# A four-engine attention and feed-forward kernel: every round of the second half gets its own order of scores, tiles, sums, jobs and evictions

## The chip, the cores and the metric

One core of one Trainium2 chip runs the whole program in one launch. The metric is the device time of that core in microseconds (us). TensorE (PE) multiplies, VectorE (DVE), ScalarE (ACT) and GpSimd (POOL) do elementwise work, SyncE (SP) issues nearly all DMAs.

## The reference

```python
x = L0_attn_X                       # (4, 1024, 256)
xn = _layernorm(x, axis=-1)
s = _L0_attn_ref(xn, Wq, Wk, Wv, Wo)    # 16 heads of 16, RoPE, causal softmax over 1024 keys
g = _silu(_L0_ffn_ref(xn, ...))         # Hadamard, 256 -> 2 x 1024, silu(gate) * up, Hadamard, -> 256
x = x + s * g
```

## The kernel before, in words

The first block (about 236 us) normalises the input, makes Q, K and V for all 4096 tokens and does the first part of the feed-forward. The second block (about 569 us) does attention and the rest of the feed-forward, woven together. This text is about the second block.

**Units.** Attention is cut into 16 units, one per batch and group of four heads. A unit takes 5 rounds (`NR`), and there are 85 rounds `z` in all: 5 that only compute maxima for unit 0, 75 in which the scores of one unit stand beside the maxima of the next, and 5 at the end with scores alone. The round's place in its unit is `r = z % 5`.

**What a round holds.** Two steps of a unit (a step is one or two blocks of 128 keys against 512 queries, at most). For each step there are two `scores`, one for each pair of heads: two matmuls side by side in the array (64 rows each), into a pair of PSUM banks. ACT takes their exponential into `probs` (`exponentials`, L1564). Then `weigh` (L1413) multiplies the probabilities by the values: four heads side by side, 32 columns of the array each, all summed in bank 7. Four `max_tile` (48 rows, L1368, some with a mask added on L1379) compute scores of the next unit whose maxima DVE reads (`read_tile`, L1681 and L1686). One or two jobs of the feed-forward (`gate`, `up`, a quarter of `down`, L343 and L353), each six matmuls on the full array, or others (`piece`, `turn`). Twice a unit, `rows` (L1426) transposes the maxima.

I name the four scores of a round S0 to S3 (S0 and S1 are the two of its first step), its tiles T0 to T3, its sums V0 (the second step of the round before) and V1 (this round's first step), its jobs J0, J1, ..., and `rows` R. The array has thus three ways in which it is divided: by rows (S and T), by columns (V), undivided (J and R). Every score, tile and job waits until the previous user of its bank has been read (`wait_banks`).

**Who is read where.** Bank 7 collects the sums of the first 512 queries (steps 0 to 2), is copied to `o_raw` by ACT (`take_heads`, L1607), and then collects those of the other 512 (steps 3 to 9). The first sum into it waits for that copy:

```python
if js[0] == 0 and QC * u + c:
    pe.wait_ge(o_taken, QC * u + c)
```

Step 2 is weighed by V1 of the round with r = 1, step 3 by V0 of the round with r = 2. So between these two sums stands one copy on ACT. Each engine goes through its list in order: an instruction that waits holds all that stands behind it.

**Orders and banks.** Six banks form three pairs (`PAIR_A`, `PAIR_B`, `PAIR_C`) for scores and tiles; jobs use single banks of a pair or bank 6. Before, the order on PE is the same in all full rounds (S0 T0 S1 V0 T1 S2 T2 J.. S3 T3 V1, with S2 ahead of T1 at r = 4), which pair each takes is fixed, ACT and DVE have orders written out in their own loops. In a round with r = 2, ACT's loop begins with `take_heads`, ahead of the exponentials.

Of the kernel before, what the change touches and what calls it, by code (L numbers as in the profile page):

```python
# [166 lines left out]

todo = []
# [5 lines left out]
SLOTS, FIRST_SLOTS, LAST_SLOTS = ((1, 1, 1, 2, 2), (4,) * NR, (1, 2, 0, 0, 0))  # L174
slots_at = lambda z: (FIRST_SLOTS if z < NR else LAST_SLOTS if z >= END else SLOTS)[z % NR]
# [30 lines left out]
PAIR_A, PAIR_B, PAIR_C = ((0, 1), (2, 3), (4, 5))  # L206
KEPT = 6
pair_of, bank_of, before_of = ({}, {}, {})

scores_first = lambda z: z % NR == NR - 1 and steps_at(z) and tiles_at(z)  # L210
holder = {bank: None for bank in range(7)}

LAST_EARLY = jobs_in(LAST, PLACES - 1)[-1]
holder[early_bank[LAST_EARLY]] = LAST_EARLY


def give(what, banks):
    before_of[what] = [x for m, x in enumerate(holder[b] for b in banks) if x and x not in [holder[b] for b in banks[:m]]]
    for bank in banks:
        holder[bank] = what  # L220


kept_open = False
for z in range(NROUND):
    if z == END + 2:
        give(('late heads', NU - 1, QC - 1), (LATE_HALVES[1][0],))

    jobs = jobs_at[z]
    if len(jobs) > 1 and jobs[0][0] == 'rows':
        jobs[0], jobs[1] = (jobs[1], jobs[0])  # L230

    if steps_at(z):
        jobs.sort(key=lambda j: j[0] == 'turn')
    now, tiles = (steps_at(z), [('tile', *t) for t in tiles_at(z)])
    s0, s1 = ([('scores', now[0], now[1] + n, p) for p in range(2)] if now else [] for n in range(2))
    early = len(jobs) if now else len(jobs) // 2

    one, other = (PAIR_B, PAIR_A) if z == NR else (PAIR_A, PAIR_B)
    for what, banks in zip(s0 + s1, (one, PAIR_C, one if scores_first(z) else other, other) if tiles
                           else (PAIR_A, PAIR_B, PAIR_A, PAIR_B)):  # L240
        pair_of[what] = banks
    pair_of.update(zip(tiles, (other, other if scores_first(z) else one, PAIR_C, PAIR_C) if now
                       else (PAIR_B, PAIR_C, PAIR_B, PAIR_C)))
    behind = s1[:1] + tiles[1:2] if scores_first(z) else tiles[1:2] + s1[:1 if tiles else 2]
    for what in s0[:1] + tiles[:1] + s0[1:] + behind + tiles[2:3 if now else 2]:
        give(what, pair_of[what])
    spare = list(one) if tiles else [4, KEPT] if z < NROUND - 1 else [KEPT, 4]
    ends_kept = kept_open or any(j[0] == 'down' for j in jobs)
    for m, j in enumerate(jobs):
        if m == early:  # L250
            for what in tiles[2:]:
                give(what, pair_of[what])
        if turn_of(j) not in bank_of:
            if j[0] == 'down' or (j[:2] != ('piece', LAST - 1) and (m == 0 or (not now and m == 3)) and not ends_kept):
                bank = KEPT
            else:
                bank = spare[0]
                spare.reverse()
            assert bank != KEPT or not kept_open
            bank_of[turn_of(j)] = bank  # L260
            give(turn_of(j), (bank,))
        if j[0] == 'down':
            kept_open = not ends_turn(j)
# [718 lines left out]
def second_block(nc, ps, io, scr, sh):  # L982
# [5 lines left out]
    with ctx:  # L988
# [69 lines left out]
        pair_round = lambda n, ib: max(job_round.get((kind, n, ib), -1) for kind in ('gate', 'up'))  # L1058

        ups = lambda z: [j for j in jobs_at[z] if j[0] in ('gate', 'up') and z == pair_round(*j[1:])  # L1060
                         and (j[0] == 'up' or ('up', *j[1:]) not in jobs_at[z])] if z >= 0 else [
                             j for j in jobs_in(LAST, PLACES - 1) if j[0] == 'up']
# [17 lines left out]
        def _(eng):  # L1080
# [95 lines left out]
            for z in range(NROUND):  # L1176
# [157 lines left out]
        def _(pe):  # L1334
# [169 lines left out]
            for z in range(NROUND):  # L1504
                now, tiles = (steps_at(z), tiles_at(z))
                if now:
                    u, s = now
                    scores(u, s, 0)
                if tiles:
                    max_tile(*tiles[0])  # L1510
                if now:
                    scores(u, s, 1)
                    if s:
                        weigh(u, s - 1)
                    elif u:
                        weigh(u - 1, NS - 1)
                if scores_first(z):
                    scores(u, s + 1, 0)
                for t in tiles[1:2]:
                    max_tile(*t)  # L1520
                if now and not scores_first(z):
                    scores(u, s + 1, 0)
                if now:
                    if not tiles:
                        scores(u, s + 1, 1)
                    for t in tiles[2:3]:
                        max_tile(*t)
                if z == NROUND - 1:
                    end_piece(0, 0)
                for m, j in enumerate(jobs_at[z]):  # L1530
                    if not now and m == len(jobs_at[z]) // 2:
                        for t in tiles[2:]:
                            max_tile(*t)
                    job(j)
                if now and tiles:
                    scores(u, s + 1, 1)
                    for t in tiles[3:]:
                        max_tile(*t)
                if now:
                    weigh(u, s)  # L1540
# [14 lines left out]
        def _(act):  # L1555
# [76 lines left out]
            for z in range(NROUND):  # L1632
                u, r = (z // NR - 1, z % NR)
                now = steps_at(z)
                if now and r == 2 and u < NU - 1:
                    take_heads(u, 0)
                if now:
# [11 lines left out]
                if now:
                    exponentials(now[0], now[1] + 1, 0)  # L1650
                for j in jobs_at[z]:
                    job(j)
                if now:
                    exponentials(now[0], now[1] + 1, 1)
# [13 lines left out]
        def _(dve):  # L1668
# [122 lines left out]
            for z in range(NROUND):  # L1791
                tiles = tiles_at(z)
                jobs = jobs_at[z]
                ahead = 3 if steps_at(z) else 2
                early = len(jobs) if steps_at(z) else len(jobs) // 2
                for t in tiles[:ahead]:
                    read_tile(*t)
# [5 lines left out]
                if z == 0:  # L1803
                    dve.memset(q_s[1][:, :, :, :].bitcast(F32), 0.0)
                for j in jobs[:early]:
                    job(j)
                for t in tiles[ahead:]:
                    read_tile(*t)
                if z == 0:
                    dve.memset(k_s[1][:, :, :, :].bitcast(F32), 1.0).then_inc(ones_set, 1)  # L1810
                for j in jobs[early:]:
                    job(j)
# [76 lines left out]
```

## Time and profile before

| what | value |
|---|---|
| time, median of 3 runs | 804.46 us (803.2 to 804.69) |
| span of the profiled execution | 804.6 us |
| busy PE / DVE / ACT / POOL | 787.2 / 566.7 / 497.8 / 411.1 us |
| first block, up to the first tile | 235.7 us |
| the 75 full rounds | about 509 us |

The profile lists the span, not another time for its own execution; the span agrees with the median within 0.02%. PE's busy time counts each matmul until its result has drained, while the next one already streams, so 98% busy doesn't mean that nothing can be gained or lost: what tells is the distance from one matmul's start to the next.

### The profile page before, as it was taken

The numbers are of one execution on the slowest core, as the hardware profiler recorded it, in microseconds if no ns is written. First come the engines' busy times: TensorE is split into PE (matmuls) and PEld (weight loads), VectorE is DVE, ScalarE is ACT, GpSimd is POOL, SyncE is SP. The second block draws the span as 40 slices with busy tenths as digits, with TensorE's granted clock in tenths as the row PEclk, the third lists the DMA queues.
The fourth block names the chain that finished last, engine by engine and source line by source line (L and its number), as shares of the span: only waits on it lengthen the run. The fifth ranks groups of instructions, "written<-read, shape, count | busy, mean of one in ns | idle before, by whom it ended". The sixth has DMA issues, their size and how long they took to land. (4 is left out here: it accounts for less than half of the span.)

```text
span 804.6 us, 14554 instructions
## 1 busy us (share of the span) xinstructions
PE 787.2 (98%) x5232; PEld 482.7 (60%) x5232; DVE 566.7 (70%) x1021; ACT 497.8 (62%) x686; POOL 411.1 (51%) x472
## 2 busy tenths in 40 slices
PE   8999999999999999999999999999999999999987
PEld 4678788888766555555555555555555555555545
DVE  5875545456686777777777777777777777777736
ACT  4576355463544777667777665677766677666472
POOL 3878678574742463321765434267453236746233
PEclk9999999999999999999999999999999999999997
DMA  9262444354541222333333453334344333445121
GB/s 319 84 199 96 158 156 158 106 131 145 182 113 39 65 77 60 91 107 107 103 107 110 122 171 93 95 108 132 115 114 142 98 105 95 133 130 170 67 87 70
DMA packets 61248, 95.71 MB, mean 119 GB/s; under 512 B 10553, under 2 KB 27641, under 8 KB 61177
## 3 DMA queue, kind: packets, MB, share of 16 engines
q1 hardware_dynamic: 59176, 92.42, 38.0%
q10 hardware_dynamic: 2000, 2.36, 0.9%
q8 instruction: 42, 0.69, 0.4%
q14 instruction: 30, 0.24, 0.1%
HBM read 57.54 MB, written 36.95 MB: 117 GB/s over the span
## 5 line engine op out<-in xcount | busy, mean ns | idle before, releaser
L1564 ACT ACTIVATE probs<-ps 128x1024 f32<-128x1024 f32 (+1 forms) x320 | 292.0, 938 | 93.7 <-PE ps L1391 92.0
L1686 DVE TENSOR_REDUCE mx<-ps 128x4 f32<-128x1024 f32 (+1 forms) x192 | 216.1, 1134 | 58.9 <-PE ps L1368 37.2
L1249 POOL TENSOR_SCALAR_AFFINE_SELECT probs<-probs 128x256 f32<-128x256 f32 (+1 forms) x192 | 92.6, 485 | 255.1 <-ACT probs L1564 254.5
L1681 DVE CUSTOM_DVE_ANT_0 ps<-ps,tri 128x512 f32<-128x512 f32 (+1 forms) x256 | 153.8, 652 | 48.4 <-PE ps L1368 48.3
L1413 PE MATMUL ps<-probs,v_ones 128*32 128x512 f32 (+3 forms) x1584 | 157.0, 486 | 0.1
L1391 PE MATMUL ps<-q_s,k_s 64*128 64x512 f32 (+3 forms) x768 | 143.7, 399 | 3.8 <-ACT probs L1564 1.4
L1368 PE MATMUL ps<-k_s,q_s 48*128 48x512 f32 (+3 forms) x768 | 134.7, 381 | 4.1 <-DVE mx L1686 0.8
L1391 PEld LDWEIGHTS ps<-q_s,k_s 64*128 64x128 f32 x768 | 67.0, 184 | 103.9 <-issue 53.6
L1368 PEld LDWEIGHTS ps<-k_s,q_s 48*128 48x128 f32 x768 | 69.5, 185 | 63.6 <-ACT probs L1564 38.2
L343 PE MATMUL ps<-xh,wug_hi 128*128 128x512 f32 x256 | 105.6, 413 | 1.0 <-DVE rot L898 1.0
L398 POOL TENSOR_TENSOR a_sb<-a_sb,u_sb 128x512 f32<-128x512 f32 x64 | 82.4, 1295 | 41.7 <-ACT u_sb L371 20.9
L343 PE MATMUL ps<-xl,wug_hi 128*128 128x512 f32 x256 | 100.1, 391 | 0.0
L343 PE MATMUL ps<-xh,wug_lo 128*128 128x512 f32 x256 | 100.1, 391 | 0.0
L411 POOL TENSOR_TENSOR hid_lo<-a_sb,hid_hi 128x512 fp32r<-128x512 f32 x64 | 83.4, 1314 | 3.5 <-ACT hid_hi L828 3.1
L384 DVE SCALAR_TENSOR_TENSOR a_sb<-a_sb,ps 128x512 f32<-128x512 f32 x64 | 43.7, 684 | 47.6 <-ACT a_sb L363 47.6
L363 ACT ACTIVATE a_sb<-ps,half_gate 128x512 f32<-128x512 f32 x64 | 44.1, 688 | 46.5 <-PE ps L343 35.6
L371 ACT ACTIVATE u_sb<-ps,half_both 128x512 f32<-128x512 f32 x64 | 44.0, 687 | 37.0 <-PE ps L343 35.7
L1413 PEld LDWEIGHTS ps<-probs,v_ones 128*32 128x32 f32 x1584 | 35.4, 108 | 45.1 <-issue 36.9
L343 PEld LDWEIGHTS ps<-xh,wug_hi 128*128 128x128 f32 x256 | 48.0, 187 | 23.6 <-issue 13.7
L353 PE MATMUL ps<-hid_hi,wd_hi 128*128 128x512 f32 x128 | 54.1, 423 | 0.6 <-POOL hid_lo L411 0.4
L343 PEld LDWEIGHTS ps<-xh,wug_lo 128*128 128x128 f32 x256 | 48.1, 188 | 10.7
L343 PEld LDWEIGHTS ps<-xl,wug_hi 128*128 128x128 f32 x256 | 48.2, 188 | 8.3
(151 smaller groups left out, 1061.5 us busy)
## 6 DMA issues: line engine op xcount, KB each, us to landing
scr_qk<-kinds SPq DMA_DIRECT2D x64, 256.0 KB, 2.4
q_s<-scr_qk SPq DMA_DIRECT2D x64, 128.0 KB, 2.8
k_s<-scr_qk SPq DMA_DIRECT2D x64, 128.0 KB, 3.0
scr_heads<-o_raw SPq DMA_DIRECT2D x30, 256.0 KB, 2.1
scr_v<-v_st SPq DMA_DIRECT2D x16, 256.0 KB, 2.9
q_s<-scr_qk SPq DMA_DIRECT2D x64, 64.0 KB, 3.0
k_s<-scr_qk SPq DMA_DIRECT2D x64, 64.0 KB, 3.1
v_raw<-scr_v SPq DMA_DIRECT2D x16, 256.0 KB, 2.8
```

Of the source, the lines that this page charges most:

```text
L343: last = pe.matmul(ps[:, bank, :], w[:, d, cols], a[:, d, :], start=m == 0, stop=m == len(terms) - 1)
L353: last = pe.matmul(ps[:, bank, :], w[:, ib, cols], h[:, ib, :], start=ib == 0 and k == 0, stop=ib == IB - 1 and k == 2)
L363: act.activation(sh.a_sb[:, m % NA, :], ps[:, bank, :], ACT.Tanh, scale=sh.half_gate[:, ib:ib + 1]).then_inc(sh.t_ok, 1)
L398: pool.tensor_tensor(sh.a_sb[:, m % NA, :], sh.a_sb[:, m % NA, :], sh.u_sb[:, m % NUP, :], op=ALU.mult).then_inc(sh.hid_ok, 1)
L411: pool.tensor_tensor(sh.hid_lo[:, ib, :], sh.a_sb[:, m % NA, :], sh.hid_hi[:, ib, :].bitcast(F32), op=ALU.subtract).then_inc(sh.hl_ok, 1)
L1249: pool.affine_select(out=part, in_=part, compare_op=ALU.is_ge, fill=0.0, base=0, pattern=pattern, channel_multiplier=-1).then_inc(cut, 1)
L1368: last = pe.matmul(ps[:, banks[e], n * w:(n + 1) * w], q[rows, i // TPC, p, i % TPC * P:(i % TPC + 1) * P], keys[rows, part, p, 0:w], star ...
L1391: last = pe.matmul(ps[:, banks[e], col:col + w], k_s[u % 2][rows, j // TPC, p, j % TPC * P:(j % TPC + 1) * P], q_s[u % 2][rows, c, p, q0:C ...
L1413: last = pe.matmul(ps[VW * h:VW * (h + 1), bank, lo:queries.stop], v_ones[u % 2][:, j, h, :], probs[:, nth_step(u, s) % 2, h // 2, h % 2, ...
L1564: act.activation(probs[:, n % 2, p, :, 0:w], ps[:, bank:bank + 2, 0:w], ACT.Exp, scale=SCALE).then_inc(exp_ok, 1)
L1681: last = dve.tensor_tensor_reduce(part_of, part_of, sh.tri[:, CH - w:CH], 1.0, LOWEST, ALU.add, ALU.max, mx[:, v % 2, kind, h, i % TPC:i % ...
L1686: last = dve.tensor_reduce(out[:, :, pairs[0]:pairs[0] + n], ps[:, banks[0]:banks[0] + 2, 0:n * w].rearrange('p e (x k) -> p e x k', x=n), ...
```

## The change

The order of every round is now a string, one for each place `r` in the unit, and one loop on each engine follows it. PE's list is the string itself. ACT's and DVE's lists are made from it: scores, rows, turns and heads go on ACT's list where they stand in the string, tiles, turns and pieces on DVE's; the evictions of gate, up and down go on ACT's list one item later and on DVE's two items later (`ACT_LAG`, `DVE_LAG`). `H` is ACT's copy of bank 7. Each score or tile takes the pair of banks that by a table of assumed durations has been free longest, and each job the bank that has. GpSimd's and SP's conditions follow the new lists. Rounds of maxima alone keep their order. `EXTRA` adds a slot only in rounds that don't occur in this size. The work, the number of matmuls and the distribution of jobs over rounds are the same.

```diff
+ORDER_F = (
+    'S0 T0 H T1 V0 S1 S2 J0 T2 J1 J2 R S3 V1 T3 J3',
+    'S0 S1 T0 V0 T1 S2 T2 H J0 R T3 S3 J1 J2 V1 J3',
+    'S0 T0 S1 V0 H T1 S2 T2 J0 T3 J1 S3 V1 J2 J3 R',
+    'S0 T0 H S1 V0 T1 S2 T2 J0 R S3 J1 T3 J2 J3 V1',
+    'S0 T0 S1 V0 T1 S2 T2 J0 J1 S3 T3 R J2 V1 J3',
+)
+ORDER_END = 'S0 S1 V0 R H S2 S3 J0 J1 J2 J3 V1'
+ACT_LAG = 1
+DVE_LAG = 2
...
+TIMES = {'tile': (220, 1500), 'scores': (220, 1400), 'gate': (1390, 600), 'up': (1390, 1400), 'weigh': (850, 0), 'rows': (60, 600),
+         'turn': (440, 1800), 'piece': (1400, 900), 'down': (1400, 2200), 'divide': (500, 1200), 'end piece': (600, 0)}
...
+def oldest(sets):
+    return min(sets, key=lambda banks: max(freed[b] for b in banks))
...
+        if what[0] in ('scores', 'rows', 'turn', 'heads'):
+            acts.append(what)
+        if what[0] in ('tile', 'turn', 'piece', 'divide'):
+            dves.append(what)
...
+        elif kind == 'H':
+            if now[1] == 4 and now[0] < NU - 1 or now[1] == 0 and now[0]:
+                new.append(('heads', now[0] - (now[1] == 0), int(now[1] == 0)))
...
             for z in range(NROUND):
                 u, r = (z // NR - 1, z % NR)
                 now = steps_at(z)
-                if now and r == 2 and u < NU - 1:
-                    take_heads(u, 0)
-                if now:
-                    for p in range(NPAIR):
-                        exponentials(*now, p)
-                if r == 0 and u >= 1:
-                    take_heads(u - 1, 1)
...
+                for m, what in enumerate(act_of[z]):
+                    if what[0] == 'scores':
+                        exponentials(*what[1:])
...
+                    elif what[0] == 'heads':
+                        take_heads(*what[1:])
```

**Place one: ACT, around the start of the round with r = 2.** `u_sb` is the eviction of a job, `probs` the exponential of one score, `o_raw0` the copy of bank 7 after step 2, `a_sb` again a job, `shift` the eviction of R. Before:

```order
L371 ACTIVATE u_sb<-ps,half_both 128x512 [waits hid_ok,up_ok]
L1564 ACTIVATE probs<-ps 128x1024 [waits pv_ok,scored]
L1607 COPY o_raw0<-ps 128x512 [waits o_out01,pv_ok]
L1564 ACTIVATE probs<-ps 128x1024 [waits pv_ok,scored] x3
L363 ACTIVATE a_sb<-ps,half_gate 128x512 [waits hl_ok,gate_ok]
L1571 ACTIVATE shift<-ps 16x128 [waits row_in01,mt_ok]
```

And now:

```order
L459 ACTIVATE u_sb<-ps,half_both 128x512 [waits hid_ok,up_ok]
L1624 ACTIVATE probs<-ps 128x1024 [waits pv_ok,scored] x3
L1667 COPY o_raw0<-ps 128x512 [waits o_out01,pv_ok]
L1624 ACTIVATE probs<-ps 128x1024 [waits pv_ok,scored]
L451 ACTIVATE a_sb<-ps,half_gate 128x512 [waits hl_ok,gate_ok]
L1624 ACTIVATE probs<-ps 128x1024 [waits pv_ok,scored]
L1631 ACTIVATE shift<-ps 16x128 [waits row_in01,mt_ok]
```

The copy has moved from ahead of S0's and S1's exponentials to behind both.

**Place two: PE at the same point.** The scores S0, the tile T0 (with its mask), the scores S1, and V0, which waits for the copy (`o_taken`). Before:

```order
L1391 MATMUL ps<-q_s0,k_s0 128x512 [waits tile_read]
L1391 MATMUL ps<-q_s0,k_s0 128x512
L1368 MATMUL ps<-k_s1,q_s1 128x256 [waits exp_ok]
L1368 MATMUL ps<-k_s1,q_s1 128x256 x3
L1379 MATMUL ps<-mask,one_hot 128x2x128 x4
L1391 MATMUL ps<-q_s0,k_s0 128x512 [waits tile_read]
L1391 MATMUL ps<-q_s0,k_s0 128x512
L1413 MATMUL ps<-probs,v_ones0 32x512 [waits o_taken,exp_ok]
```

And now:

```order
L1476 MATMUL ps<-q_s0,k_s0 128x512 [waits tile_read]
L1476 MATMUL ps<-q_s0,k_s0 128x512
L1453 MATMUL ps<-k_s1,q_s1 128x256 [waits tile_read]
L1453 MATMUL ps<-k_s1,q_s1 128x256 x3
L1464 MATMUL ps<-mask,one_hot 128x2x128 x4
L1476 MATMUL ps<-q_s0,k_s0 128x512 [waits exp_ok]
L1476 MATMUL ps<-q_s0,k_s0 128x512
L1498 MATMUL ps<-probs,v_ones0 32x512 [waits o_taken,exp_ok]
```

PE's own order here is unchanged; only whose read a bank waits for differs.

**Place three: PE, from the end of the round with r = 0 into that with r = 1.** The tile T3 of r = 0 is the pair of `128x384` on the first line below; V1 is `32x512`, S0 is the first `128x256`, and the tile T0 of r = 1 is the `128x128`. Before:

```order
L1368 MATMUL ps<-k_s1,q_s1 128x384 [waits tile_read]
L1368 MATMUL ps<-k_s1,q_s1 128x384
L1413 MATMUL ps<-probs,v_ones0 32x512 [waits v_set,o_taken,cut,exp_ok]
L1413 MATMUL ps<-probs,v_ones0 32x512 x3
L1391 MATMUL ps<-q_s0,k_s0 128x256 [waits tile_read,shift_ok]
L1391 MATMUL ps<-q_s0,k_s0 128x256
L1391 MATMUL ps<-q_s0,k_s0 128x128 x2
L1368 MATMUL ps<-k_s1,q_s1 128x128 [waits exp_ok,qk_in11]
```

And now (V1 stands first, T3 behind it):

```order
L1498 MATMUL ps<-probs,v_ones0 32x512 [waits v_set,o_taken,cut,exp_ok]
L1498 MATMUL ps<-probs,v_ones0 32x512 x3
L1453 MATMUL ps<-k_s1,q_s1 128x384 [waits exp_ok,shift_ok]
L1453 MATMUL ps<-k_s1,q_s1 128x384
L1476 MATMUL ps<-q_s0,k_s0 128x256 [waits tile_read]
L1476 MATMUL ps<-q_s0,k_s0 128x256
L1476 MATMUL ps<-q_s0,k_s0 128x128 x2
L1476 MATMUL ps<-q_s0,k_s0 128x256 [waits exp_ok]
L1476 MATMUL ps<-q_s0,k_s0 128x256
L1476 MATMUL ps<-q_s0,k_s0 128x128 x2
L1453 MATMUL ps<-k_s1,q_s1 128x128 [waits tile_read,qk_in11]
```

T3 has moved behind V1, S1 ahead of T0, and T0 now waits for a tile's read (`tile_read`), that of this same T3, whose pair it takes, where it waited for an exponential.

## Rows read from the trace of the kernel before

**Rows 1.** The page: busy us, share of the span, instructions.

```profile
PE 787.2 (98%) x5232; PEld 482.7 (60%) x5232; DVE 566.7 (70%) x1021; ACT 497.8 (62%) x686; POOL 411.1 (51%) x472
```

**Rows 2.** Windows: us, busy time of each engine, PEclk, DMA share, GB/s.

```profile
235.70:253.70 18.00, 16.47 (x75) 11.43 (x74) 12.68 (x26) 4.44 (x8) 0.00 (x0) 0.91 0.18 59
253.70:763.00 509.30, 505.05 (x3782) 270.67 (x3782) 388.75 (x738) 348.05 (x454) 236.68 (x315) 1.00 0.37 107
```

**Rows 3.** Timeline of PE alone, tile and scores into a job.

```profile
302.18 0.41 PE L1391 MATMUL ps<-q_s,k_s 64*128 64x512 f32 x2
302.41 0.40 PE L1368 MATMUL ps<-k_s,q_s 48*128 48x512 f32 x2
302.74 0.50 PE L343 MATMUL ps<-xh,wug_hi 128*128 128x512 f32 x1
303.08 0.39 PE L343 MATMUL ps<-xl,wug_hi 128*128 128x512 f32 x1
303.31 0.39 PE L343 MATMUL ps<-xh,wug_lo 128*128 128x512 f32 x1
```

**Rows 4.** Timeline of PE's weight loads at the same place.

```profile
302.26 0.19 PEld L1368 LDWEIGHTS ps<-k_s,q_s 48*128 48x128 f32 x2
302.74 0.19 PEld L343 LDWEIGHTS ps<-xh,wug_hi 128*128 128x128 f32 x1 [0.29 <-issue]
302.85 0.19 PEld L343 LDWEIGHTS ps<-xl,wug_hi 128*128 128x128 f32 x1
```

**Rows 5.** Timeline, start of a round with r = 2.

```profile
366.36 0.50 PE L1391 MATMUL ps<-q_s,k_s 64*128 64x512 f32 x2
366.50 0.59 ACT L1607 COPY o_raw<-ps 128x512 f32<-128x512 f32 x1 [0.22 <-PE ps L1413]
366.98 1.95 ACT L1564 ACTIVATE probs<-ps 128x1024 f32<-128x1024 f32 x2
367.28 0.50 PE L1391 MATMUL ps<-q_s,k_s 64*128 64x512 f32 x2
367.71 1.07 PE L1413 MATMUL ps<-probs,v_ones 128*32 128x512 f32 x8
...
368.70 0.50 PE L1368 MATMUL ps<-k_s,q_s 48*128 48x512 f32 x2
```

**Rows 6.** Timeline, a score whose exponential starts on an idle ACT.

```profile
373.09 0.50 PE L1391 MATMUL ps<-q_s,k_s 64*128 64x512 f32 x2
373.62 1.94 ACT L1564 ACTIVATE probs<-ps 128x1024 f32<-128x1024 f32 x2 [0.56 <-PE ps L1391]
```

**Rows 7.** Timeline, T3 of a round with r = 0 and its read.

```profile
358.90 0.44 PE L1368 MATMUL ps<-k_s,q_s 48*128 48x384 f32 x2
359.38 0.57 DVE L1681 CUSTOM_DVE_ANT_0 ps<-ps,tri 128x384 f32<-128x384 f32 x1 [0.54 <-PE ps L1368]
359.86 0.60 DVE L1681 CUSTOM_DVE_ANT_0 ps<-ps,tri 128x384 f32<-128x384 f32 x1
360.38 0.14 DVE L1681 DVE_READ_ACCUMULATOR2_ANT mx<- 128x1 f32 x1
```

**Rows 8.** Waits, whole span: us in total, times, longest.

```profile
PEld ps L1368 <- DVE mx L1686: 7.5, 24, 1.0
PEld ps L1391 <- DVE mx L1681: 6.4, 20, 0.6
PEld ps L1368 <- DVE mx L1681: 2.9, 8, 0.9
PEld ps L1391 <- DVE mx L1686: 2.6, 9, 0.4
```

**Rows 9.** Windows before and in the one stretch of a lower clock.

```profile
238.00:239.00 1.00, 0.50 (x2) 0.19 (x2) 1.00 (x4) 0.31 (x1) 0.00 (x0) 1.00 0.70 262
239.00:240.00 1.00, 0.55 (x3) 0.36 (x4) 1.00 (x4) 0.00 (x0) 0.00 (x0) 1.00 0.05 8
241.00:242.00 1.00, 1.00 (x4) 0.81 (x3) 1.00 (x2) 0.00 (x0) 0.00 (x0) 0.50 0.79 268
```

More of the change, by code:

```diff
@@ L203 @@
 LAST_FEATURES = max(z for j, z in job_round.items() if j[0] in ('gate', 'up'))
-PAIR_A, PAIR_B, PAIR_C = ((0, 1), (2, 3), (4, 5))
+PAIRS = [(0, 1), (2, 3), (4, 5)]
+PAIR_A, PAIR_B, PAIR_C = PAIRS
 KEPT = 6
 pair_of, bank_of, before_of = ({}, {}, {})
-scores_first = lambda z: z % NR == NR - 1 and steps_at(z) and tiles_at(z)
-holder = {bank: None for bank in range(7)}
+holder = {bank: None for bank in range(8)}
 LAST_EARLY = jobs_in(LAST, PLACES - 1)[-1]
 holder[early_bank[LAST_EARLY]] = LAST_EARLY
+freed = {bank: 0 for bank in range(8)}
+freed[early_bank[LAST_EARLY]] = 1500
+TIMES = {'tile': (220, 1500), 'scores': (220, 1400), 'gate': (1390, 600), 'up': (1390, 1400), 'weigh': (850, 0), 'rows': (60, 600),
+         'turn': (440, 1800), 'piece': (1400, 900), 'down': (1400, 2200), 'divide': (500, 1200), 'end piece': (600, 0)}
+clock = 0
 def give(what, banks):
@@ L220, in give, with until @@
         holder[bank] = what
+def oldest(sets):
+    return min(sets, key=lambda banks: max(freed[b] for b in banks))
+def until(banks, kind):
+    for b in banks:
+        freed[b] = clock + sum(TIMES[kind])
+order_of, act_of, dve_of = ([], [], [])
+late_act, late_dve = ([], [])
 kept_open = False
 for z in range(NROUND):
+    now, tiles = (steps_at(z), tiles_at(z))
+    v, r = divmod(z, NR)
     if z == END + 2:
         give(('late heads', NU - 1, QC - 1), (LATE_HALVES[1][0],))
-    jobs = jobs_at[z]
@@ L229 @@
[L229 to L263, printed above, removed]
@@ L264 @@
-    if not jobs and not now:
-        for what in tiles[2:]:
-            give(what, pair_of[what])
-    if now:
-        for what in (s1[1:] if tiles else []) + tiles[3:]:
-            give(what, pair_of[what])
+    rows = [j for j in jobs_at[z] if j[0] == 'rows']
+    others = [j for j in jobs_at[z] if j[0] != 'rows']
+    if now:
+        others.sort(key=lambda j: j[0] == 'turn')
+    shape = ORDER_T[r] if not now else ORDER_END if not tiles else ORDER_F[r]
+    order, acts, dves = ([], [], [])
@@ new lines, in take @@
+    def take(what):
+        order.append(what)
+        for late in (late_act, late_dve):
+            for x in late:
+                x[0] -= 1
+        for late, to in ((late_act, acts), (late_dve, dves)):
+            while late and late[0][0] <= 0:
+                to.append(late.pop(0)[1])
+        if what[0] in ('scores', 'rows', 'turn', 'heads'):
+            acts.append(what)
+        if what[0] in ('tile', 'turn', 'piece', 'divide'):
+            dves.append(what)
+    turn_pairs = [PAIR_A, PAIR_B]
@@ new lines @@
+    order_of.append(order)
+    act_of.append(acts)
+    dve_of.append(dves)
+assert not late_act and not late_dve
+gated_round = {what: z for z in range(NROUND) for what in dve_of[z] if what[0] in ('gate', 'down')}
+taken_round = {what: z for z in range(NROUND) for what in act_of[z] if what[0] in ('up', 'gate')}
+pool_round = {}
+for j in list(taken_round):
+    if j[0] == 'up':
+        pool_round[j] = max(taken_round[j], gated_round.get(('gate', *j[1:]), 0))
+assert sum(j[0] == 'down' for z in range(END, NROUND) for j in jobs_at[z]) <= 3
@@ L1056, in second_block @@
         block = ctx.enter_context(nc.Block())
[L1058 to L1062, printed above, removed]
+        ups = lambda z: sorted([j for j, at in pool_round.items() if at == z], key=lambda j: nth_hid(*j[1:])) if z >= 0 else [
+            j for j in jobs_in(LAST, PLACES - 1) if j[0] == 'up']
         nth_x = lambda n: n - NEARLY - 1
@@ L1504, in _ @@
             for z in range(NROUND):
-                now, tiles = (steps_at(z), tiles_at(z))
-                if now:
[L1507 to L1540, printed above, removed]
+                for what in order_of[z]:
+                    if what[0] == 'tile':
+                        max_tile(*what[1:])
+                    elif what[0] == 'scores':
+                        scores(*what[1:])
+                    elif what[0] == 'weigh':
+                        weigh(*what[1:])
+                    elif what[0] == 'end piece':
+                        end_piece(*what[1:])
+                    elif what[0] != 'heads':
+                        job(what)
             end_piece(0, 1)
@@ L1634, in _ @@
                 now = steps_at(z)
-                if now and r == 2 and u < NU - 1:
-                    take_heads(u, 0)
-                if now:
-                    for p in range(NPAIR):
-                        exponentials(*now, p)
-                if r == 0 and u >= 1:
-                    take_heads(u - 1, 1)
-                if at(z, 'high') is not None and at(z, 'high') < LAST - 1:
-                    high_part(at(z, 'high'))
                 if z < NR:
                     normalise_at(z)
-                if z < NR:
                     for j in ups(z - 1):
                         hidden_high(*j[1:])
[L1649 to L1654, printed above, removed]
+                n_scores = 0
+                for m, what in enumerate(act_of[z]):
+                    if what[0] == 'scores':
+                        exponentials(*what[1:])
+                        n_scores += 1
+                        if n_scores == 2 and at(z, 'high') is not None and at(z, 'high') < LAST - 1:
+                            high_part(at(z, 'high'))
+                    elif what[0] == 'heads':
+                        take_heads(*what[1:])
+                    else:
+                        job(what)
                 if z == NR:
@@ L1802, in _ @@
                     low_part(LAST - 1)
[L1803 to L1812, printed above, removed]
+                for n, what in enumerate(dve_of[z]):
+                    if what[0] == 'tile':
+                        read_tile(*what[1:])
+                    else:
+                        job(what)
+                    if z == 0 and n == 1:
+                        dve.memset(q_s[1][:, :, :, :].bitcast(F32), 0.0)
+                    if z == 0 and n == 3:
+                        dve.memset(k_s[1][:, :, :, :].bitcast(F32), 1.0).then_inc(ones_set, 1)
                 if z == NR:
```

77 lines of the change are left out of this document (68 added, 9 removed), and 5 rows, old and new, of the table ORDER_T.

## The prediction, made before the changed kernel ran

> **What bounds the kernel now.** The page first: PE is busy 98% of the span, DVE 70%, ACT 62%, POOL 51% [rows 1]. The windows say where: in the 75 full rounds, 509.3 us, PE is busy 505.05 us and its clock is granted in full [rows 2]. Busy there is no proof of work, because a matmul counts until it has drained. So I went to the timeline and read starts. Inside a job, matmuls start every 0.23 us (303.08, 303.31); a tile behind a score also follows at 0.23 us (302.18, 302.41), its load under the matmul ahead [rows 3, 4]. Where the division of the array changes, from the tile to the job, the next start comes after 0.33 us, and the one behind it after 0.34 us [rows 3]. The load explains it: the job's first load starts together with its first matmul at 302.74, instead of under the one before, while the second load already starts at 302.85, under the first matmul [rows 4]. So one change of division costs 0.10 + 0.11, about 0.2 us.
>
> The order lists 491 such changes in the second block, 447 of them in the full rounds: 447 x 0.2 = 89 us of 509. What else is lost on PE are waits for a read bank. Those that DVE ends sum to 7.5 + 6.4 + 2.9 + 2.6 = 19.4 us in 61 waits, none over 1.0 us [rows 8]; part of each is the load that would have been late anyway. Streaming alone I estimate at 388 us for these rounds (the columns in the order, at 0.23 us for 512, and 0.80 for a V of 512, which is the 1.0 us from 367.71 to the next start at 368.70 [rows 5] less one change). 509 - 388 - 89 leaves 32 us for waits of every size. That is the most an order can win back. PE's list is therefore the bound, and other engines matter where PE waits for them.
>
> **The change, part by part.** Three things differ on PE: how often the division changes, which read each item waits for, and when the reads come.
>
> *Changes of division.* In an ordinary unit the old order changes 6 times in each of the five rounds, 30 in all. The new strings give 9, 5, 7, 8 and 6, so 35: at r = 0 a tile stands behind the job and R stands alone behind that tile, at r = 2 R stands behind V1, at r = 3 the second job is parted from the first. Over the whole program I count 571 for 491: 80 more, x 0.2 us [rows 3] = **+16 us**. Nothing hides this, since it lies on PE itself. The Trainium skill, page "TensorEngine Tiling (Array Packing)", section "Key Properties", says that changing the tiling mode drains the TensorE. If a change exposed a whole drain and load, the price from rows would be (0.39 - 0.23) + 0.19 = 0.35 us [rows 3, 4] and the part 28 us; the starts in the trace show 0.2, and the sum goes by them.
>
> *The copy of bank 7.* On PE, V0 at r = 2 is the first sum into bank 7 after the copy. Today the copy starts at 366.50, 0.14 us after S0, and has ended at 367.09; V0 starts at 367.71, 1.35 us after S0, and doesn't feel it [rows 5]. In the new ACT list the copy stands behind the exponentials of S0 and S1. With S0 at 0: its exponential begins at 0.53, which is the distance from a score to its exponential on an idle ACT (373.09 to 373.62) [rows 6]; two exponentials take 1.95 [rows 5], so the copy begins at 2.48 and ends at 3.07; with 0.1 for the semaphore V0 starts at 3.17. 3.17 - 1.35 = 1.82 us, and V0 has nothing to go past it: T1, S2, T2 and the job stand behind it on PE. This comes in units 0 to 14 (the last unit's copy is DVE's and stays), 15 x 1.82 = **+27 us**. The store of the heads (SP) starts some 2.4 us later; their loads stand rounds away, so I cost it at nothing, and if one did wait it would be ACT's next copy in the same bank of `o_raw`, five rounds on.
>
> *The tile T0 at r = 1.* Today T3 of r = 0 is followed by V1, S0, and T0 takes the pair of a score; it is S1 that takes T3's pair. In the new order T3 is behind V1, then S0 and S1 of the next round take the two older pairs, and T0 is left with T3's. In the trace, that tile starts at 358.90, DVE reads it from 359.38 to 360.52 in two passes [rows 7]: 1.62 us from start to free, and 0.05 to PE, 1.67. In the new order T0 would start after T3 itself (0.17 for 384 columns, 0.11 for its late load) and two scores of 384 columns (0.17 each, as r = 1 uses step 2): 0.62. So PE waits 1.05 us, and the load after such a wait is late too (0.11). 15 times 1.16 = **+17 us**. It holds if DVE is at T3 when it arrives: T2 and the gate's eviction stand ahead of it, and the string puts 2 us of PE work (R, S3, V1) between T2 and T3. V0 is queued behind T0; its exponentials are done by then, so nothing is late beyond PE.
>
> *The waits that go.* The old tile T3 waited for T2's pair, two places back, and similar tiles now wait for T1's. At r = 3 and 4 little is waited for before or after. The 19.4 us of [rows 8] lie mostly in the rounds with r = 0 and 1. And each of the two new waits lets DVE and ACT catch up. I take **-12 us**, between 0 and the 32 us above, nearer to the part of [rows 8] that isn't late load.
>
> *At nothing.* R at r = 2 goes behind V1, so its eviction on ACT and the two small DMAs on SP go about 2 us later; the scores that need those rows are two rounds, some 13 us (509.3 / 75 each), away, and that SP order also holds the next unit's load, which has as long. R at r = 0 keeps its distance to the scores that need it. ACT's job evictions stand one item later, DVE's gates about where they stood, and POOL, at 236.68 busy of 509.30 [rows 2], has room for what it gets later; if it had none, V1's mask step would hold PE. Rounds of maxima and the first block don't change. More instructions on the lists than before: none that compute.
>
> **Sum.** Against the profiled execution's span of 804.6 us (the median is 804.46, the same within the measurement): 804.6 + 16 + 27 + 17 - 12 = 852.6, so **852 us**, 6% slower.
>
> **The rivals.**
> - *Forecast: both waits and the changes are paid.* 840 to 866 us. Chance 0.60.
> - *One new wait is smaller than it looks.* If DVE reads T3 at once and waits of every size go, T0's 17 us vanish: 804.6 + 16 + 27 - 32 = 816 at the least, and 836 with 12 won back. For it: the old waits are all short [rows 8]. Against it: a bank cannot be written before 1.67 us, and 0.62 us of work stands between. Chance 0.17, 816 to 840.
> - *The clock falls.* The one stretch with half the clock in the second block comes behind two slices in which PE was busy 0.50 and 0.55 [rows 9]. The wait at r = 2 leaves PE idle for about 1.8 us in 3.2. Around that stretch the clock's mean over 18 us is 0.91 [rows 2], so the dip cost 0.09 x 18 = 1.6 us of work. In all 15 units that gives +24, 876 us; in some, 866 to 876. Against it: the new stalls are shorter than that dip's and stand between full stretches. Chance 0.16.
> - *Other side: not slower.* Only if the copy is no wait. The point is 1.35 us after S0: if the copy ends by then, V0 doesn't notice. That needs ACT to be done with both exponentials 0.8 us after S0, while one takes 0.97 [rows 5]; or PE to be so late at V0 for another reason that the wait is covered. With T0's wait covered too and all 32 us won back, 804.6 + 16 - 32 = 789 us. Chance 0.05.
> - *The evenly spread order wins as much as it costs* (16 + 27 + 17 = 60 against at most 32): would need twice the waits that there are. Chance 0.02, about 804.
>
> **How the numbers follow.** The forecast is that of the likeliest case, 852. The range takes the case with one smaller wait down to 830 and that of the clock up to 874; about 2 in 10 is left outside. A measurement here tells 0.2% (1.6 us) from no change. Faster by more: 0.05; within: 0.02; slower: 0.93.
>
> **What the changed profile would show.** Copy: in a round with r = 2, the `o_raw` copy behind a pair of exponentials, and V0 about 3.2 us after S0; among PE's waits a new group ended by ACT's copy, 15 times, each up to 1.8 us. Tile: a group ended by DVE's second pass over a 384-column tile, 15 times, about 1 us. Changes: the distance of 0.33 where the job or R is parted from its like. Rounds: r = 2 longer by 1.6 to 2 us, r = 1 by about 0.5 to 1, r = 0 by some 0.2, r = 4 the same. Busy times of DVE, ACT and POOL nearly as before. I would be wrong if V0 at r = 2 still starts within 1.5 us of S0, or if the rounds with r = 3 and 4, which get no long wait, change by more than 0.5 us.

## The result and the profile after

| | before | after |
|---|---|---|
| median of 4 runs | 804.46 us (803.2 to 804.69) | 862.97 us (856.74 to 866.82) |
| span of the profiled execution | 804.6 us | 858.0 us, own time 859.69 |
| clock granted to PE, mean over the span | 0.993 | 0.988, in the other three runs 0.977, 0.991 and 0.98 |

The ratio is 1.0724, with an interval from 1.0672 to 1.0775: 58.5 us slower by the medians, where 48 were forecast, and inside the range. The runs of after spread over 10 us, those of before over 1.5, and the runs with the lower clock are the long ones.

The page of after, busy time and share, against [rows 1]:

```profile
PE 800.4 (93%) x5232; PEld 483.7 (56%) x5232; DVE 570.0 (66%) x1021; ACT 503.1 (59%) x686; POOL 411.3 (48%) x472
```

The other engines do what they did, and all have more idle time. PE is busy 93% instead of 98%, so this time waits are long enough to show as idle PE. The waits of after, those of PE's matmuls and what is left of the four groups of [rows 8]:

```profile
PE ps L1498 <- ACT o_raw L1667: 26.9, 15, 1.9
PE ps L1453 <- DVE mx L1736: 16.6, 17, 1.7
PEld ps L1453 <- DVE mx L1741: 4.0, 17, 0.4
PEld ps L1453 <- DVE mx L1736: 3.4, 2, 2.0
PEld ps L1476 <- DVE mx L1736: 1.6, 4, 0.7
PEld ps L1476 <- DVE mx L1741: 0.4, 1, 0.4
```

Two groups are new: sums (L1498) that wait for ACT's copy, 15 times, and tiles (L1453) that wait for DVE's second pass, 17 times. Fifteen of the 17 are T0 at r = 1, 0.92 us each and 13.7 us together; the other two, 2.8 us with the longest of 1.7, stand in the rounds of maxima. The four groups of weight loads that DVE ended before, 19.4 us, are down to 9.4. The start of a round with r = 2 in after, to be laid beside [rows 5]:

```profile
379.00 0.50 PE L1476 MATMUL ps<-q_s,k_s 64*128 64x512 f32 x2
...
379.54 1.94 ACT L1624 ACTIVATE probs<-ps 128x1024 f32<-128x1024 f32 x2 [0.20 <-PE ps L1476]
...
379.87 0.48 PE L1476 MATMUL ps<-q_s,k_s 64*128 64x512 f32 x2
...
381.36 0.59 ACT L1667 COPY o_raw<-ps 128x512 f32<-128x512 f32 x1
382.10 1.07 PE L1498 MATMUL ps<-probs,v_ones 128*32 128x512 f32 x8 [1.75 <-ACT o_raw L1667]
```

S0 at 379.00, exponentials from 379.54 to 381.48, the copy right behind, V0 at 382.10: 3.10 us after S0, where it was 1.35. And the end of the round with r = 0, to be laid beside [rows 7]:

```profile
371.90 0.45 PE L1453 MATMUL ps<-k_s,q_s 48*128 48x384 f32 x2
372.18 0.57 PE L1476 MATMUL ps<-q_s,k_s 64*128 64x256 f32 x8
372.38 0.57 DVE L1736 CUSTOM_DVE_ANT_0 ps<-ps,tri 128x384 f32<-128x384 f32 x1 [0.81 <-PE ps L1453]
...
373.67 0.44 PE L1453 MATMUL ps<-k_s,q_s 48*128 48x128 f32 x4 [0.91 <-DVE mx L1736]
```

T3 starts at 371.90 and T0, which takes its banks, at 373.67, 1.77 us later; it is so in all 15 units. Between them PE had two scores to do and nothing else.

The windows of the 75 full rounds and of the rest (columns as in [rows 2]; before, 253 to 763, they took 510 us):

```profile
255.80:819.80 564.00, 520.64 (x3783) 273.53 (x3782) 389.62 (x738) 354.04 (x454) 236.56 (x314) 0.98 0.33 97
819.80:858.00 38.20, 33.10 (x279) 18.17 (x275) 22.66 (x33) 20.27 (x27) 13.94 (x20) 0.99 0.24 82
```

The loss of the profiled execution, 53.4 us, lies in the full rounds, which take 54 us more; outside them the rounds of maxima take 2.8 us more and the end some 3.5 less. Laid out by the starts of their first matmuls, the rounds of a unit last, on the mean, in us:

| | r = 0 | r = 1 | r = 2 | r = 3 | r = 4 |
|---|---|---|---|---|---|
| before | 6.38 | 6.40 | 6.61 | 7.54 | 7.07 |
| after | 6.46 | 7.14 | 8.97 | 7.93 | 7.11 |

The clock has a part that the forecast left out. Windows of after around one of its stretches at half the clock:

```profile
455.00:456.00 1.00, 0.00 (x0) 0.00 (x0) 0.99 (x1) 1.00 (x2) 0.73 (x2) 1.00 0.00 0
456.00:457.00 1.00, 0.15 (x4) 0.18 (x8) 0.00 (x0) 0.70 (x2) 0.00 (x0) 1.00 0.14 32
457.00:458.00 1.00, 1.00 (x10) 0.16 (x5) 0.00 (x0) 0.00 (x0) 0.00 (x0) 1.00 0.41 62
...
459.00:460.00 1.00, 1.00 (x4) 0.77 (x3) 1.00 (x2) 0.84 (x1) 0.00 (x0) 0.50 1.02 338
460.00:461.00 1.00, 1.00 (x3) 0.72 (x3) 0.75 (x1) 0.00 (x0) 0.00 (x0) 0.50 0.66 207
```

PE waits for the copy in 455 and 456, does one sum, and from about 458 runs at 1.2 GHz for 3.4 us, which loses at most half of that, 1.7 us. The profiled execution has five such stretches inside the full rounds, each behind such a wait, 5 x 1.7 = 8.5 us at most; the five rounds with r = 2 that hold one last about 9.97 us, the ten others 8.47. The full rounds of before have none.

Two mistakes of the first part. The one stretch of a lower clock that it shows is not the only one in the second block of before: the last rounds have another, of 10.1 us from 796.5, and the window from 763 to the end has a granted clock of 0.90. And the table gives 235.7 us as the first tile. That is the first tile of the fourth round of maxima. The view of the tile reads says 212.7:

```profile
L1686 DVE TENSOR_REDUCE mx<-ps x192: 622/1223/1229, 212.7 to 762.3; 128x2 f32<-128x1024 f32 x128, 128x4 f32<-128x512 f32 x32, 128x4 f32<-128x1024 f32 x32
```

No term of the sum used either.

### The profile page after: what moved, and what is told of

It reads as the page before. It is cut to its first block, busy times and chain, and to the rows that moved or that the text cites. A ratio compares the mean times of both kernels' runs of the same rounds, so it can differ in the third digit from the quotient of the medians.

```text
span 858.0 us, 14562 instructions
## 1 busy us (share of the span) xinstructions
PE 800.4 (93%) x5232; PEld 483.7 (56%) x5232; DVE 570.0 (66%) x1021; ACT 503.1 (59%) x686; POOL 411.3 (48%) x472
## 4 chain that ended last, share of the span: by engine, by line
PE 62%; DVE 5%; ACT 4%; issue 3%; POOL 0%; DVEq 0%; ACTq 0%
PE ps L1498 16%; PE ps L431 13%; PE ps L1453 12%; PE ps L1476 9%; PE ps L441 7%; PE ps L1539 3%; ACT probs L1624 3%; DVE ps L1736 3%; PE ps L1464 1%; ACT o_raw L1667 1%; PE ps L1511 1%; DVE mx L1741 1%; DVE xl L1752 0%; PE ps L1555 0%; DVE mx L1736 0%
## 5 line engine op out<-in xcount | busy, mean ns | idle before, releaser
L1498 PE MATMUL ps<-probs,v_ones 128*32 128x512 f32 (+3 forms) x1584 | 158.9, 491 | 27.3 <-ACT o_raw L1667 26.9
L1453 PE MATMUL ps<-k_s,q_s 48*128 48x512 f32 (+3 forms) x768 | 144.7, 402 | 18.3 <-DVE mx L1736 16.6
L1453 PEld LDWEIGHTS ps<-k_s,q_s 48*128 48x128 f32 x768 | 70.7, 187 | 115.8 <-issue 77.9
L1476 PE MATMUL ps<-q_s,k_s 64*128 64x512 f32 (+3 forms) x768 | 133.3, 385 | 1.6 <-ACT probs L1624 0.8
L431 PE MATMUL ps<-xh,wug_hi 128*128 128x512 f32 x256 | 109.3, 427 | 1.3 <-DVE rot L986 1.0
L431 PE MATMUL ps<-xl,wug_hi 128*128 128x512 f32 x256 | 101.9, 398 | 0.0
L1498 PEld LDWEIGHTS ps<-probs,v_ones 128*32 128x32 f32 x1584 | 35.7, 108 | 75.6 <-ACT probs L1624 36.1
```

What stands on the lines that cost most here:

```text
L431: last = pe.matmul(ps[:, bank, :], w[:, d, cols], a[:, d, :], start=m == 0, stop=m == len(terms) - 1)
L1453: last = pe.matmul(ps[:, banks[e], n * w:(n + 1) * w], q[rows, i // TPC, p, i % TPC * P:(i % TPC + 1) * P], keys[rows, part, p, 0:w], star ...
L1476: last = pe.matmul(ps[:, banks[e], col:col + w], k_s[u % 2][rows, j // TPC, p, j % TPC * P:(j % TPC + 1) * P], q_s[u % 2][rows, c, p, q0:C ...
L1498: last = pe.matmul(ps[VW * h:VW * (h + 1), bank, lo:queries.stop], v_ones[u % 2][:, j, h, :], probs[:, nth_step(u, s) % 2, h // 2, h % 2, ...
```

## The experiments

**copy_first: the copy back ahead of the exponentials at r = 2.**

```diff
-    'S0 T0 S1 V0 H T1 S2 T2 J0 T3 J1 S3 V1 J2 J3 R',
+    'H S0 T0 S1 V0 T1 S2 T2 J0 T3 J1 S3 V1 J2 J3 R',
```

> The changed kernel with one item moved: in rounds with r = 2, H (ACT's copy of bank 7) stands first, ahead of S0, as in the kernel before. Theory (the copy behind two exponentials holds V0 by 1.8 us in 15 rounds): the group of PE waits ended by the o_raw copy, 26.9 us in 15 waits, goes to nothing, rounds with r = 2 get 1.8 us shorter (8.97 to about 7.1), and the time falls by about 27 us, to some 835. If the stretches of half clock are brought on by these waits, it falls by up to 10 us more, and the granted clock is nearer to 0.993. Rival (the array's changes of division and the other wait carry the loss, and the copy's wait only covers others that then appear): under 15 us less, over 848.

824.19 us (823.02 to 826.49), ratio to before 1.0266 (1.0244 to 1.0287): 39 us less than after for one letter moved. The 15 waits for the copy are gone, and the tile's are untouched:

```profile
PE ps L1453 <- DVE mx L1736: 16.5, 17, 1.7
```

Rounds with r = 2 last 6.63 us, before's 6.61. The clock's mean is 1.0, 0.998, 0.995 and 1.0 in its four runs, and none of the full rounds has a stretch at half. Between the profiled spans, 858.0 - 821.3 = 36.7 us, 35.0 of them in the full rounds, where 26.9 of waits and up to 8.5 of clock make 35.4. The rest fits a stretch at half that after has in its rounds of maxima (222.7 us) and this run has not.

**before_copy_late: the same edit in the kernel before, the other way round.**

```diff
-                if now and r == 2 and u < NU - 1:
-                    take_heads(u, 0)
                 if now:
                     for p in range(NPAIR):
                         exponentials(*now, p)
+                if now and r == 2 and u < NU - 1:
+                    take_heads(u, 0)
```

> The kernel before, with one edit: in rounds with r = 2, ACT's copy of bank 7 behind the exponentials of S0 and S1, as the change has it. Nothing else is changed. Theory: 15 x 1.82 = 27 us more, 832, V0 3.2 us after S0, and perhaps some us of half clock on top (up to 840). Rival (the waits that the old order has anyway are covered by this one, and DVE and ACT catch up in it): under 15 us more.

845.4 us (842.69 to 849.84), ratio 1.0525 (1.0485 to 1.0566), 42 us more than its 803.42. The wait is as large as expected, V0 starts 3.10 us after S0, and the clock takes more than I allowed:

```profile
PE ps L1413 <- ACT o_raw L1607: 27.4, 15, 1.9
```

The clock's mean falls to 0.984, 0.977, 0.971 and 0.983. The profiled execution has seven stretches at half in the full rounds, 7 x 1.7 = 12 us: 27 + 12 = 39 of the 42. The rival falls: the old order's short waits don't cover it.

**copy_middle: the copy behind one exponential instead of two.**

```diff
-    'S0 T0 S1 V0 H T1 S2 T2 J0 T3 J1 S3 V1 J2 J3 R',
+    'S0 H T0 S1 V0 T1 S2 T2 J0 T3 J1 S3 V1 J2 J3 R',
```

> The changed kernel with the copy at r = 2 between the exponentials of S0 and S1, so that it is behind one exponential and not two. Theory: V0 about 2.2 us after S0 in place of 3.17, PE's wait for the copy 15 x 0.9 = 13 us in place of 26.9. If the clock falls because of the 1.8 us wait, the clock should stay up with the 0.9 us wait: 863 - 14 - 8 to 12 = about 838 to 841. Rival (the clock falls with the half wait too): 849.

838.86 us (836.43 to 840.28), ratio 1.043 (1.0409 to 1.045). The wait has half its size, as said:

```profile
PE ps L1498 <- ACT o_raw L1667: 13.2, 15, 1.0
```

And the clock stays up: 0.998, 0.997, 0.996, 1.0, with no stretch at half in the full rounds. So at this place 15 waits of up to 1.0 us cost themselves and nothing more, while 15 of up to 1.9 us also bring the clock down in some of the units.

**t3_ahead: T3 ahead of V1 at r = 0.**

```diff
-    'S0 T0 H T1 V0 S1 S2 J0 T2 J1 J2 R S3 V1 T3 J3',
+    'S0 T0 H T1 V0 S1 S2 J0 T2 J1 J2 R S3 T3 V1 J3',
```

> The changed kernel with T3 back ahead of V1 in rounds with r = 0, so that 1 us of sums stands between T3 and the tile that takes its banks. Theory: PE's waits ended by DVE's pass over a 384-column tile (16.6 us in 17) go; T3 itself now takes the banks of R, 0.4 us of work behind it, and waits some 0.3 us, 15 times, so of 17 us about 12 come back: some 851. Rival (the tile's wait lies beside another that is as long): under 4 us less.

856.67 us (854.21 to 858.15), ratio 1.0657 (1.0636 to 1.0679): 6 us under after by the medians, between the 12 of the theory and the 4 of the rival, with nine stretches at half in the full rounds instead of five. The tile's wait shrinks from 16.6 us to 5.0:

```profile
PE ps L1453 <- DVE mx L1736: 5.0, 9, 1.7
```

Of these 5.0 us, 2.8 are the two waits in the rounds of maxima, so T0's 15 fell from 13.7 us to 2.2. The full rounds of the two profiled executions differ by only 1.8 us; the four stretches more cost up to 1.7 us each, so without the clock the edit is worth some 8. The clock's mean is 0.979 to 0.985 in the runs of this kernel. The clean measure of this edit is the next run.

**both_mended: both edits.**

> Both edits together: H first at r = 2, T3 ahead of V1 at r = 0. The 571 changes of division stay. Theory: no long wait is left, and what remains over the kernel before is 80 changes of 0.2 us less whatever the new bank choice wins: 863 - 27 - 12 - up to 10 of clock = 814 to 824, above 804.5 by 10 to 20. Rival (changes of division cost nothing in a stream that waits anyway; the two waits are all): 800 to 806.

816.88 us (814.85 to 818.54), ratio 1.0164 (1.014 to 1.0188), clock 0.996 to 1.0. This is inside the 814 to 824 expected. Against copy_first the tile's edit is worth 7 us, not 12. T3's weight load now waits 0.24 us for R's banks, of which 0.09 shows from start to start, and T0 still waits for T3's read in 7 of the 15 units, 0.47 us each and 0.2 on the mean. Around them S1 and V0 of r = 1 come another 0.10 and 0.07 us later. What is left over before, 13 us, is what the 80 extra changes of division cost (16 us at 0.2) and these waits, less what was won back.

**old_order: the new code with the old strings.**

```diff
-    'S0 T0 H T1 V0 S1 S2 J0 T2 J1 J2 R S3 V1 T3 J3',
-    'S0 S1 T0 V0 T1 S2 T2 H J0 R T3 S3 J1 J2 V1 J3',
-    'S0 T0 S1 V0 H T1 S2 T2 J0 T3 J1 S3 V1 J2 J3 R',
-    'S0 T0 H S1 V0 T1 S2 T2 J0 R S3 J1 T3 J2 J3 V1',
-    'S0 T0 S1 V0 T1 S2 T2 J0 J1 S3 T3 R J2 V1 J3',
+    'S0 T0 S1 H V0 T1 S2 T2 J0 R J1 J2 J3 S3 T3 V1',
+    'S0 T0 S1 V0 T1 S2 T2 J0 J1 J2 J3 S3 T3 V1',
+    'H S0 T0 S1 V0 T1 S2 T2 J0 R J1 J2 J3 S3 T3 V1',
+    'S0 T0 S1 V0 T1 S2 T2 J0 J1 J2 J3 S3 T3 V1',
+    'S0 T0 S1 V0 S2 T1 T2 J0 J1 J2 J3 S3 T3 V1',
```

> The changed kernel's code with the strings of the kernel before (J's and R joined, S3 T3 V1 last, H where ACT's loop had the copy: behind S1 at r = 0, first at r = 2). PE's order is nearly that of before, with 492 changes of division; what stays of the change is the choice of banks by age and the lists of ACT and DVE. Theory: the old kernel's time less a few short waits, 797 to 804. Rival (bank choice and eviction lists are themselves a loss): over 806.

803.29 us (801.94 to 805.74, 12 runs), ratio 0.9993 (0.9983 to 1.0003): the same as before. With the old strings, choosing banks by age and making ACT's and DVE's lists from the string cost and win nothing in sum. By rounds, r = 1 falls from 6.40 to 6.12, because T3 there takes the pair of an item one place older, and r = 2 rises from 6.61 to 6.74, because S1 now waits for a tile's read; the first five rounds take some us more, the last five less, with a different share of half clock in each.

**old_split: two cuts in old_order, R behind V1 at r = 2, the second job behind S3 at r = 3.**

```diff
-    'H S0 T0 S1 V0 T1 S2 T2 J0 R J1 J2 J3 S3 T3 V1',
-    'S0 T0 S1 V0 T1 S2 T2 J0 J1 J2 J3 S3 T3 V1',
+    'H S0 T0 S1 V0 T1 S2 T2 J0 J1 J2 J3 S3 T3 V1 R',
+    'S0 T0 S1 V0 T1 S2 T2 J0 S3 J1 J2 J3 T3 V1',
```

> As old_order, with two cuts: R behind V1 at r = 2, and the second job behind S3 at r = 3. 535 changes of division for 492, 43 more, and no new long wait (the nearest read, R's, lies 0.88 us behind). Theory: 43 x 0.2 = 8.6 us over old_order. Rival 1 (a change costs the whole drain and load, 0.35 us): 15 us. Rival 2 (a stream that waits anyway absorbs the change): under 3 us.

813.68 us (812.98 to 815.89), ratio 1.0117 (1.0097 to 1.0136), 10.4 us over old_order for 43 changes, 0.24 us each if all of it were theirs. The place with the parted job (PE alone):

```profile
382.84 0.40 PE L431 MATMUL ps<-xh,wug_lo 128*128 128x512 f32 x1
383.17 0.51 PE L1476 MATMUL ps<-q_s,k_s 64*128 64x512 f32 x2
383.60 0.50 PE L431 MATMUL ps<-xh,wug_hi 128*128 128x512 f32 x1
383.94 0.39 PE L431 MATMUL ps<-xl,wug_hi 128*128 128x512 f32 x1
384.17 0.39 PE L431 MATMUL ps<-xh,wug_lo 128*128 128x512 f32 x1
```

S3, alone between two jobs, takes 0.43 us (383.17 to 383.60) for 0.23 us of streaming, and is 0.33 behind the job's last start in place of 0.23; the next job's first matmul takes 0.34. That is 0.10 + 0.20 + 0.11 = 0.41 us for two more changes, 0.2 us each.

The 10.4 us also hold a wait that the expectation had ruled out. With R behind V1, T0 at r = 3 takes the pair of T3 of the round before. In 6 of the 15 units it starts 0.84 us behind S0 in place of 0.34, and the group that this makes is missing in old_order:

```profile
PE ps L1453 <- DVE mx L1741: 2.0, 6, 0.3
...
482.33 0.49 PE L1476 MATMUL ps<-q_s,k_s 64*128 64x512 f32 x2
483.16 0.50 PE L1453 MATMUL ps<-k_s,q_s 48*128 48x256 f32 x4 [0.34 <-DVE mx L1741]
```

These are 6 x 0.5 = 3.0 of the 10.4 us. What is left, 7.4 us for 43 changes, is 0.17 us each: the parted job pays 0.2 for each of its changes, and R behind V1 less. Rival 2 falls, and rival 1, a whole drain and load at 0.35 us, is too high: 15 us would lie outside the interval of this run.

**joined: an attempt at a better order, with nothing parted.**

```diff
+    'S0 T0 H T1 V0 S1 S2 T2 J0 R J1 J2 S3 T3 V1 J3',
+    'S0 T0 S1 V0 T1 S2 T2 J0 R J1 J2 T3 S3 V1 J3',
+    'H S0 T0 S1 V0 T1 S2 T2 J0 R J1 J2 T3 S3 V1 J3',
+    'S0 T0 S1 V0 T1 S2 T2 J0 J1 J2 J3 T3 S3 V1',
```

> An attempt at a better order: the changed kernel's strings with the copy first at r = 2 and everything joined that it parted: T2 ahead of the job, S3 and T3 ahead of V1, R in the jobs, 495 changes of division. T3 goes ahead of S3 at r = 1, 2 and 3, so that it takes the banks of an item two places back. Theory: the waits of both_mended without its extra changes, 817 - 76 x 0.2 = 802, or a few us below the kernel before if the tile's waits that the old order has go. Rival: no gain over old_order.

815.75 us (813.86 to 818.36), ratio 1.0147 (1.0126 to 1.0169). The theory was wrong, and the rival, no gain, didn't say that it would be 12 us worse than before. At r = 0 it waits in a new place:

```profile
361.56 0.69 DVE L1736 CUSTOM_DVE_ANT_0 ps<-ps,tri 128x512 f32<-128x512 f32 x1
...
362.16 0.73 DVE L1736 CUSTOM_DVE_ANT_0 ps<-ps,tri 128x512 f32<-128x512 f32 x1
...
363.01 0.44 PE L1453 MATMUL ps<-k_s,q_s 48*128 48x384 f32 x2 [0.52 <-DVE mx L1736]
```

T2 stands right behind S1 and S2 and takes the pair of T1. T1's read can begin only when T0's has ended and takes two passes, so T2 starts 0.80 us behind S2 on the mean, where 0.23 would do: 0.57 us, 15 times, 8.6 us. In after the job stands between S2 and T2 and covers it: two changes of division, 0.4 us, are the price of that. This is not all. Against old_order, r = 0 is longer by 0.39 us, r = 1 by 0.21 and r = 3 by 0.20, the last by the same wait of T0 as in old_split.

**maxima_mended: old_order with the old banks and R's old place in the five rounds of maxima.**

> old_order, with the banks (and R's place) of the kernel before in the five rounds that hold maxima alone, where old_order reaches the first full round at 258.0 us and the kernel before at 253.1. Everything behind is old_order's. Theory (the bank choice by age costs those rounds up to 5 us, and wins about 2 in the full ones): 803.3 - 3 to 5 = 798 to 800, under the kernel before. Rival (the 5 us are the clock's phase or the place in the trace, not the banks): 802 to 804.

803.61 us (802.18 to 805.79, 12 runs), ratio 0.9991 (0.9979 to 1.0004): no gain, as the rival said. By the start of its first score, the first full round begins at 256.7 us, in old_order at 257.6 and in before at 253.0. The clock in the rounds ahead of it is 0.92 in both new runs, with two stretches at half, and 0.96 in before, with one. That stretch accounts for 1.7 us of the 3.7; beside the rest stand two waits for a tile's read, of 1.28 and 1.14 us, where before has 0.77 and 0.54. So the lead of before is the clock only in part, and what else makes it was not tested. In the totals the long stretch at half in the last rounds of before's profiled execution goes the other way. It also follows that the rounds of maxima did not stay as they were, as the first part says: R has another place in one of them, the banks differ, and in after they hold the two waits of 2.8 us together.

**t2_behind: maxima_mended with T2 behind the job at r = 0, nothing parted.**

```diff
-    'S0 T0 S1 H V0 T1 S2 T2 J0 R J1 J2 J3 S3 T3 V1',
+    'S0 T0 H T1 V0 S1 S2 J0 R J1 J2 T2 S3 T3 V1 J3',
```

> maxima_mended with the string at r = 0 changed to S0 T0 H T1 V0 S1 S2 J0 R J1 J2 T2 S3 T3 V1 J3: T2 behind the job instead of ahead of it, still 492 changes. In old_order T2 waits 0.2 us and T3 0.17 us there, in the changed kernel, where T2 stands behind the job, neither. T3 now takes R's banks 0.5 us behind it. Theory: about 0.3 us a unit better, 4 us under maxima_mended, 795. Rival (R's eviction or T2's read then holds T3 or the next S0): no better than maxima_mended.

810.57 us (809.09 to 811.16), ratio 1.0077 (1.0061 to 1.0092). A miss, and the rival told where: T2's wait is gone, T3 waits for R's banks in 8 of 15 units (2.1 us of idle PE), and at r = 1 the score S1, which takes T3's pair, starts 0.67 us behind T0 instead of 0.46. The likely reason, not tested, is that T2 and T3 now reach DVE one behind the other. r = 1 lasts 6.46 us instead of 6.12.

## Why the prediction was right, point by point

**The copy of bank 7, +27 us.** Right: 26.9 us in 15 waits, V0 3.10 us after S0 for 3.17. That it agrees to the tenth is luck. The starting point of 1.35 us was that of one unit, and the 15 units of before lie at 1.14 to 1.35, 1.22 on the mean, so by starts V0 came 1.89 us later and not 1.82; on the other side the copy started 0.1 us earlier than worked out. copy_first and before_copy_late show the term from both sides, and copy_middle shows that it scales with what stands ahead of the copy.

**The tile T0 at r = 1, +17 us.** The working holds: T0 starts 1.77 us after T3, where the prediction had 1.67 and 0.11 for the late load, and 0.62 us of work stands between, so 15 x 1.15 = 17. The profile counts 13.7 us of idle PE for it, since a matmul counts as busy until it has drained; that the whole group reads 16.6 comes from two waits elsewhere. Its worth to the whole was less: both_mended is 7 us under copy_first, because T0 still waits in 7 units and T3 and its neighbours come a little later. The mechanism is shown; the edit removes only a part of the wait, so the 17 us were not measured alone.

**Changes of division, +16 us.** Not contradicted: the starts in old_split give 0.2 us for each change around the parted job, and the time 0.17 on the mean once the 3.0 us of T0's new waits are taken off; 0.24, which the time gives as it stands, is an upper bound. So 80 changes are 14 to 19 us. The rule that a change of the tiling mode drains the TensorE (the Trainium skill, page "TensorEngine Tiling (Array Packing)", section "Key Properties") has the right direction, and no price; the traces show that the load behind a change comes late, and a drain and a load in full, 0.35, would be too much.

**The waits that go, -12 us.** For the profiled execution: 54 in the full rounds = 16 + 27 + 17 + 8.5 of clock - x, so x is about 14. Read at the weight loads, DVE's four groups fell by 10. Both lie in the range from 0 to 32. r = 0 shows it: three more changes, 0.6 us, and the round is longer by only 0.08. The reading behind this term was loose: of the 19.4 us of [rows 8], the rounds with r = 0 and 1 hold 9 and not most, and r = 4 alone 4.9.

**At nothing.** "Rounds of maxima don't change" was wrong by 2.8 us, and the end of the program, 3.5 us shorter and with less half clock, hid it. r = 3 and 4 changed by 0.39 and 0.04 us, within the 0.5 that was set as a sign of being wrong; two changes at r = 3 are 0.4.

**The clock.** This is the term that was missing. I had it as a rival (24 us if every wait brings it down, 866 to 876 if some do, chance 0.16) and at nothing in the forecast. The runs show a share: five stretches in the profiled execution, 8.5 us at most, and two runs of 866 us with a clock of 0.977 and 0.98. With it the profiled span closes: 852 + 8.5 - the 2 us that the winnings exceeded mine is 858 or 859 for 858.0. Since the winnings were found as a remainder, this is a check of consistency and not a proof. That not every wait brings the clock down fits the spread of 10 us between runs of one program. That these long waits are the cause is shown by copy_first, copy_middle and before_copy_late. What decides it at a given wait stays open, and length alone doesn't: waits of 1.1 to 1.3 us in the rounds of maxima also stand right ahead of a stretch at half, as here in old_order, where the clock falls at 243.9:

```profile
243.57 0.46 PE L1453 MATMUL ps<-k_s,q_s 48*128 48x384 f32 x2 [1.14 <-DVE mx L1736]
243.96 0.79 PE L441 MATMUL ps<-hid_hi,wd_hi 128*128 128x512 f32 x1
244.55 0.63 PE L441 MATMUL ps<-hid_lo,wd_hi 128*128 128x512 f32 x1
```

On the other side copy_first has a wait of 1.67 us at 221.7 with no stretch behind it, where after has one of 1.68 us at the same place and a stretch from 222.7.

**The sign.** The argument that carried it was a bound: the order could win back no more than about 32 us (a remainder over an estimate of the streaming time), and 60 stood against that.

## What to carry to other kernels

When an order is rewritten, list for each engine what a waiting instruction now stands behind, above all the rare items such as one copy in five rounds: a single copy moved behind two exponentials cost 39 of 58 us, with what it took in clock. Price each regrouping twice, by the changes of division that it adds (about 0.2 us each here) and by the reads that it brings too near; a read needs its whole queue's time, with what stands ahead of it on the reading engine. A wait near 2 us in a dense stream of matmuls can cost its own length and part of it again in clock, while 15 of up to 1 us in the same place didn't. When a cut is priced by its time alone, look whether it brought a wait with it, as it did in old_split.

## What was not expected of the hardware

The clock fell behind waits of 1.7 to 1.9 us that stood between stretches in which PE was fully busy, in 5 to 9 of 15 places, differently from run to run (0.971 to 0.991 on the mean), and never behind the 15 waits of 0.8 to 1.0 us at the same place in the profiled execution of copy_middle. In the rounds of maxima single waits of 1.1 to 1.7 us stood ahead of a stretch in some executions and not in others. Each of these stretches at 1.2 GHz lasted 3.4 us and cost 1.5 to 1.7.
